# A fused decoder layer on one core: attention scores as three single-pass products, with the instruction lists written anew

## The reference, cut to what matters

```python
x = _layernorm(x + _L0_attn_ref(x, ...))                 # mixer
x = _layernorm(x + _L0_xattn_ref(ctx_1024, x, ...))      # attention
x = _layernorm(x + _L0_ffn_ref(x, ...))                  # three cycles
# the attention, 8 heads of 64; 120 context rows + 256 own rows = 376 keys
kv_input = jnp.concatenate([xn, ln], axis=-2)
q, k, v = (to_heads(q) * scale, to_heads(k), to_heads(v))
sim = jnp.einsum('bhid,bhjd->bhij', q, k)                # 256 x 376 scores a head
attn = jax.nn.softmax(sim, axis=-1)
out = jnp.einsum('bhij,bhjd->bhid', attn, v)
```

## Time and profile before

| | |
|---|---|
| median of 3 runs | 3804.09 us |
| profiled execution | 3802.06 us, of which the span is 3800.1 us |
| granted TensorE clock | mean 0.992; 1.00 (2.4 GHz) from 100 us on |
| busy in the span | PE 98%, PEld 79%, DVE 85%, ACT 87%, POOL 48% |
| DMA | 203 MB, 53 GB/s, 18% of the 16 DMA engines |

### The profile page before, as it was taken

The page is one execution under the profiler, slowest core; times in us unless marked ns, Lnnn a source line. Parts: engine busy times, 40 slices in busy tenths (PEclk is TensorE's granted clock), DMA queues, the critical chain, the costliest instruction groups (busy, mean ns, idle before and its releaser), DMA issues.

```text
span 3800.1 us, 77874 instructions
## 1 busy us (share of the span) xinstructions
PE 3718.5 (98%) x25728; PEld 2996.7 (79%) x25728; DVE 3248.2 (85%) x8098; ACT 3304.6 (87%) x7875; POOL 1810.0 (48%) x3084
## 2 busy tenths in 40 slices
PE   5999999999999999999999999999999999999996
PEld 4788887878878878888878788788888888787875
DVE  7888888888988888888888888888888888888874
ACT  5888988988888889889889898898898898888985
POOL 4355455454454554554554544545545545445442
PEclk8999999999999999999999999999999999999998
DMA  3111211212212212112112122121121121221210
GB/s 103 57 57 41 65 49 49 60 44 60 59 39 65 59 39 65 57 42 65 42 57 60 42 62 59 39 65 58 41 65 56 43 64 40 59 60 39 65 29 20
DMA packets 312353, 203.17 MB, mean 53 GB/s; under 512 B 55056, under 2 KB 310928, under 8 KB 311952
## 3 DMA queue, kind: packets, MB, share of 16 engines
q1 hardware_dynamic: 311952, 198.20, 18.0%
HBM read 180.17 MB, written 17.96 MB: 52 GB/s over the span
## 4 chain that ended last, share of the span: by engine, by line
PE 75%; ACT 19%; issue 2%; DVE 2%; POOL 1%; SPq 0%; DMA 0%; POOLq 0%; DVEq 0%; ACTq 0%
PE psum L254 28%; PE psum L453 9%; PE psum L429 8%; PE psum L439 7%; PE psum L464 6%; PE psum L498 5%; PE psum L326 5%; ACT prob L986 3%; PE psum L504 2%; ACT L986 2%; ACT L1028 2%; ACT L878 2%; PE psum L513 1%; ACT h L1028 1%; ACT gate L929 1%
## 5 line engine op out<-in xcount | busy, mean ns | idle before, releaser
L986 ACT ACTIVATE prob<-psum,nmax 128x376 f32<-128x376 f32 x1024 | 585.9, 573 | 60.6 <-DVE nmax L1686 57.2
L1686 DVE TENSOR_REDUCE nmax<-psum 128x1 f32<-128x376 f32 x1024 | 539.1, 537 | 36.7 <-PE psum L429 32.1
L2440 POOL TENSOR_TENSOR Lm<-Lm,G 128x384 f32<-128x384 f32 x512 | 526.9, 1064 | 87.2 <-DVE out_sb L1814 67.7
L439 PE MATMUL psum<-ident,prob 128*128 128x128 f32 (+1 forms) x3072 | 509.9, 278 | 3.3 <-ACT probT L996 1.1
L439 PEld LDWEIGHTS psum<-ident,prob 128*128 128x128 f32 (+1 forms) x3072 | 359.6, 143 | 169.5 <-issue 36.8
L1453 DVE SCALAR_TENSOR_TENSOR u<-psum,par,u 128x255 f32<-128x255 f32 (+5 forms) x960 | 440.0, 476 | 44.0 <-ACT u L888 29.5
L429 PE MATMUL psum<-kT,q_sb 64*128 64x376 f32 x2048 | 464.5, 528 | 0.0
L1709 DVE COPY probT<-psum 128x384 f32<-128x384 f32 x512 | 281.2, 549 | 125.5 <-PE psum L439 121.5
L2495 POOL TENSOR_TENSOR h_a<-h_a,cpl 128x512 f32<-128x512 f32 x64 | 82.3, 1285 | 611.0 <-DVE h_pre L1797 611.0
L254 PE MATMUL psum<-x_hi,w_in_hi 128*128 128x256 f32 (+1 forms) x1152 | 342.1, 297 | 26.5 <-DVE u L1453 15.3
L453 PE MATMUL psum<-probT,V 128*64 128x256 f32 (+1 forms) x3072 | 360.7, 383 | 0.6 <-DVE probT L1709 0.6
(11 more groups left out here) (220 smaller groups left out, 11350.5 us busy)
## 6 DMA issues: line engine op xcount, KB each, us to landing
Lm<-cum_row SPq DMA_DIRECT2D x64, 1024.0 KB, 5.2
Lm<-cum_row SPq DMA_DIRECT2D x64, 512.0 KB, 6.5
invT<-inv_row SPq DMA_DIRECT2D x256, 128.0 KB, 3.1
xT_sb<-in_xT SPq DMA_DIRECT2D x64, 256.0 KB, 2.9
x_sb<-in_x SPq DMA_DIRECT2D x64, 256.0 KB, 2.9
result<-out_sb SPq DMA_DIRECT2D x64, 256.0 KB, 2.2
inv_row<-inv_t SPq DMA_DIRECT2D x512, 1.0 KB
ctx_sb<-in_ctx SPq DMA_DIRECT2D x64, 120.0 KB, 4.2
```

The source lines that it names most:

```text
L439: t = tr(banks[b][0:m, j * P:(j + 1) * P], prob[:, r, j0:j0 + m], ident[:, :])
L986: act(prob[:, r, :], b[:, 0:NK], ACT.Exp, bias=nmax[:, n:n + 1], accum_out=psum_row[:, n:n + 1]).then_inc(a_exp, 1)
L1686: e.tensor_reduce(nmax[:, n:n + 1], banks[bank_of["sc", s, n]][:, 0:NK], AX.X, ALU.max, negate=True).then_inc(d_max, 1)
L2440: t = tt(Lm[:, h, :], Lm[:, h, :], G[:, :], ALU.mult)
```

## The change

- Scores: `k_out` and `q_out` now write float32r halves `k_hi` and `q_hi`; VectorE gets two new helpers, `k_low` (4 a sequence, 376 columns) and `q_low` (2 a sequence, 512 columns), which write the low halves and release the bank. `scores` makes three float32r products for each head, six matmuls in place of two, and tells of both tiles with one semaphore.
- `top` reduces the two tiles of a call at once (8 a sequence on 2 x 376 columns). `exp` stays at 16.
- `ring_s` has four banks, 0 to 3; the network's banks come from `ring_m`.
- `y_pair` puts two calls in one bank, and `values` does two pairs of heads with one bank and one release; `values_out` copies 512 columns, twice a sequence.
- `x1_pre` is gone: `x1_sum` writes into `x1[s % 2]`, which `x1_keep` normalises in place. `xT_sb` shares its memory with `x_lo`, and `kv` with `kv_lo`; `ctx_n` is `ctx_sb`, and `x_sb` is single. The loads and the copies that write them wait for later events.
- All lists of all engines are written in a new order.

```diff
+        def shared(name, other, shape):
+            at = -(-nc.sbuf_base // 32) * 32
+            t = sb(name, shape, F32R)
+            slices = tuple(slice(None) for _ in shape)
+            return t, nc.alloc_sbuf_tensor_at(other, shape, F32, offset=at)[slices]
...
-        xT_sb, x_sb = sb("xT_sb", [P, KT, L]), sb("x_sb", [P, 2, TT, D])
+        x_sb = sb("x_sb", [P, TT, D])
...
-        kv, kv_hi, kv_lo = sb("kv", [P, KT, NK]), sb("kv_hi", [P, KT, NK], F32R), sb("kv_lo", [P, KT, NK], F32R)
-        q_sb, kT = sb("q_sb", [P, CT, L]), sb("kT", [P, CT, NK])
+        kv_hi, (kv_lo, kv) = sb("kv_hi", [P, KT, NK], F32R), shared("kv_lo", "kv", [P, KT, NK])
+        q_hi, q_lo = sb("q_hi", [P, CT, L], F32R), sb("q_lo", [P, CT, L], F32R)
+        k_hi, k_lo = sb("k_hi", [P, CT, NK], F32R), sb("k_lo", [P, CT, NK], F32R)
...
-            ring_s, ring_b, ring_m = [1, 2, 3], list(ring_turn), [6, 7]
+            ring_s, ring_b, ring_m = [0, 1, 2, 3], list(ring_turn), [6, 7]
...
             def k_tile(s, c):
...
-                freed[b] = [(a_k, 4 * s + c + 1)]
+                freed[b] = [(d_kl, 4 * s + c + 1)]
...
             def scores(s, c, i):
-                pe.wait_ge(a_q, 2 * s + c // 2 + 1)
-                pe.wait_ge(a_k, 4 * s + c + 1)
+                pe.wait_ge(d_ql, 2 * s + c // 2 + 1)
+                pe.wait_ge(d_kl, 4 * s + c + 1)
+                at = [take(ring_s), take(ring_s)]
+                bank_of["sc", s, n // 2] = at[0]
+                assert at[1] == at[0] + 1
+                for m, (q_, k_) in enumerate(((q_hi, k_hi), (q_lo, k_hi), (q_hi, k_lo))):
+                    for k in range(2):
+                        r = slice(k * HD, (k + 1) * HD)
+                        t = mm(banks[at[k]][:, 0:NK], q_[r, c, i * P:(i + 1) * P], k_[r, c, :], start=m == 0, stop=m == 2)
+                t.then_inc(p_sc, 1)
                 for k in range(2):
-                    b = bank_of["sc", s, n + k] = take(ring_s)
-                    r = slice(k * HD, (k + 1) * HD)
-                    mm(banks[b][:, 0:NK], q_sb[r, c, i * P:(i + 1) * P], kT[r, c, :], start=True, stop=True).then_inc(p_sc, 1)
-                    freed[b] = [(a_exp, 16 * s + n + k + 1)]
+                    freed[at[k]] = [(a_exp, 16 * s + n + k + 1)]
...
             def layer(s, cyc, n):
-                b = wait_free(0)
+                at = bank_of["f", s, cyc, n] = take(ring_m)
+                b = banks[at]
...
-                act(oT[:, c, :], b[:, 0:L], ACT.Copy).then_inc(a_o, 1)
+                act(oT[:, 2 * d:2 * d + 2, :], b[:, :].rearrange("p (c t) -> p c t", c=2), ACT.Copy).then_inc(a_o, 1)
...
+            def q_low(s, j):
+                ve.wait_ge(a_q, 2 * s + j + 1)
+                tt(q_lo[:, 2 * j:2 * j + 2, :], b[:, :].rearrange("p (c t) -> p c t", c=2),
+                   q_hi[:, 2 * j:2 * j + 2, :].bitcast(F32), ALU.subtract).then_inc(d_ql, 1)
+            def k_low(s, c):
+                ve.wait_ge(a_k, 4 * s + c + 1)
+                tt(k_lo[:, c, :], banks[bank_of["k", s, c]][:, 0:NK], k_hi[:, c, :].bitcast(F32), ALU.subtract).then_inc(d_kl, 1)
...
-                e.tensor_reduce(nmax[:, n:n + 1], banks[bank_of["sc", s, n]][:, 0:NK], AX.X, ALU.max, negate=True).then_inc(d_max, 1)
+                e.tensor_reduce(nmax[:, 2 * n:2 * n + 2], psum[:, b:b + 2, 0:NK], AX.X, ALU.max, negate=True).then_inc(d_max, 1)
...
             def load_xT(s):
-                sp.wait_ge(d_xlo, s)
+                sp.wait_ge(p_bcdt, s)
+                sp.wait_ge(p_x, 2 * s)
+                sp.wait_ge(p_z, 2 * s)
```

More of the change, by code:

```diff
@@ new lines, in _ @@
+                v_tile(f, 0)
+                cb(a)
+                in_z(a, 1)
+                turn(f, 0)
+                w_o(f - 1, 0)
+                w_o(f - 1, 1)
+                turn(f, 1)
+                scores(f, 1, 0)
+                scores(f, 1, 1)
+                turn(f, 2)
+                q_pair(f, 1)
+                y_pair(a, 0)
+                y_pair(a, 1)
+                y_pair(a, 2)
+                y_pair(a, 3)
+                scores(f, 2, 0)
+                bcdt(m)
@@ new lines, in _ @@
+                k_tile(f, 3)
+                in_x(m, 0)
+                v_tile(f, 1)
+                x2_turn(f - 1)
+                turn(f, 3)
+                scores(f, 2, 1)
+                scores(f, 3, 0)
+                turn(f, 4)
+                turn(f, 5)
+                mean_square(a)
+                out_proj(a)
+                layer(f - 1, 0, 0)
+                v_tile(f, 2)
+                ctxT(a)
+                layer(f - 1, 0, 1)
+                turn(f, 6)
+                glob(f - 1, 0)
@@ L621, in _ @@
+                turn(f, 7)
+                layer(f - 1, 0, 2)
+                glob(f - 1, 1)
+                scores(f, 3, 1)
+                turn(f, 8)
+                glob(f - 1, 2)
+                twisted(f - 1)
+                layer(f - 1, 0, 3)
+                turn(f, 9)
+                turn(f, 10)
+                x1T(a)
+                in_x(m, 1)
+                values(f, 0)
+                k_tile(a, 0)
+                layer(f - 1, 1, 1)
+                q_pair(a, 0)
                 layer(f - 1, 1, 2)
@@ L685, in _ @@
-                values(a, 0)
-                values(a, 1)
-                q_pair(m, 0)
-                layer(f, 1, 1)
-                turn(a, 10)
-                k_tile(m, 0)
-            last = NSEQ - 1
+            last = NSEQ - 1
+            values(last - 3, 1)
+            layer(last - 4, 2, 3)
+            cb(last - 1)
+            v_tile(last - 2, 0)
+            in_z(last - 1, 1)
+            scores(last - 2, 1, 0)
+            turn(last - 2, 0)
+            w_o(last - 3, 0)
+            q_pair(last - 2, 1)
@@ new lines, in _ @@
+            w_o(last - 3, 1)
+            scores(last - 2, 1, 1)
+            y_pair(last - 1, 0)
+            y_pair(last - 1, 1)
+            scores(last - 2, 2, 0)
+            y_pair(last - 1, 2)
+            y_pair(last - 1, 3)
+            bcdt(last)
+            turn(last - 2, 1)
+            turn(last - 2, 2)
+            in_x(last, 0)
+            k_tile(last - 2, 3)
+            v_tile(last - 2, 1)
+            x2_turn(last - 3)
+            turn(last - 2, 3)
+            scores(last - 2, 2, 1)
@@ new lines, in _ @@
+            scores(last - 2, 3, 0)
+            turn(last - 2, 4)
+            turn(last - 2, 5)
+            mean_square(last - 1)
+            out_proj(last - 1)
+            layer(last - 3, 0, 0)
+            turn(last - 2, 6)
+            v_tile(last - 2, 2)
+            ctxT(last - 1)
+            layer(last - 3, 0, 1)
+            turn(last - 2, 7)
+            turn(last - 2, 8)
+            glob(last - 3, 0)
+            layer(last - 3, 0, 2)
+            glob(last - 3, 1)
+            scores(last - 2, 3, 1)
@@ L692, in _ @@
+            glob(last - 3, 2)
+            twisted(last - 3)
+            layer(last - 3, 0, 3)
+            turn(last - 2, 9)
+            turn(last - 2, 10)
+            x1T(last - 1)
+            in_x(last, 1)
+            values(last - 2, 0)
+            k_tile(last - 1, 0)
+            layer(last - 3, 1, 1)
+            q_pair(last - 1, 0)
             layer(last - 3, 1, 2)
             k_tile(last - 1, 1)
+            layer(last - 3, 1, 3)
+            turn(last - 2, 11)
             xcT(last, 0)
-            layer(last - 3, 1, 3)
+            xcT(last, 1)
@@ L707, in _ @@
             layer(last - 3, 2, 2)
-            values(last - 2, 2)
-            values(last - 2, 3)
-            scores(last - 1, 0, 1)
-            turn(last - 1, 0)
+            values(last - 2, 1)
             layer(last - 3, 2, 3)
@@ new lines, in _ @@
+            conv_tap(last, 2, 2)
+            k_low(last - 1, 0)
+            x_silu(last, 0)
+            q_low(last - 1, 0)
+            x_silu(last, 1)
+            out_stats(last - 4, 0)
+            k_low(last - 1, 1)
+            gain(last - 3, 1)
+            x_dt(last, 0)
+            twisted_part(last - 3, 1)
+            turn_inverse(last - 2, 1)
+            pre(last - 3, 1)
+            turn_out(last - 2, 12)
+            k_low(last - 1, 2)
+            top(last - 1, 0)
+            x_dt(last, 1)
```

1578 lines of the change are left out of this document (733 added, 845 removed).

## The result

The changed kernel takes 3687.03 us (median of 4 runs, 3685.63 to 3689.21), the kernel before 3804.62 (4 runs, 3803.94 to 3806.9): ratio 0.969, 95% interval 0.9674 to 0.9707. It is 117.6 us faster.

What follows compares the result with a forecast made beforehand. PE, full of work, was taken as the bound: 3802 us less 96 (products 64, shapes 32) plus 32 of new waits gives 3738, forecast as a median of 3740 us, range 3690 to 3840.

Steps and rivals of the forecast that it cites:

- Products, 64 us: Score calls on PE: three rounds of float32r products at 0.17 us, saving 0.125 us a call, 64 us in all.
- Both float32r rivals: Score calls slower: float32r halves don't run abreast (3969 us, chance 5%), or each round shows its weight load (3998, 2%).
- The lists at 32 us: New order of PE's loop: 15 changes of array shape a sequence instead of 18, saving 32 us (0 to 45).
- PE, fewer changes of shape: Prediction's step on PE's loop: three fewer changes of array shape a sequence at 0.165 us each, 32 us saved.
- no room for a wait: PE's timeline before the change: matmul starts follow so closely that PE is full of work, 57.9 us a sequence.
- Waits, +32 us: PE waiting for DVE's new low halves at scores and banks: 0.5 us a sequence more, 32 us (0 to 141).
- more gain: Rival on PE: rounds of 0.157 us, no new waits, bank waits gone; 3675 to 3690 us, chance 6%.
- ACT at nothing: ScalarE: 236 us of table loads and 23 of values_out copies come off, but none counts in the sum.
- DVE +142 us: VectorE: k_low adds 138 us, q_low 87, merged maxima take 83 off; net 142, 94% busy.
- DVE's waits eat the gain: Rival: PE's gain is eaten by waits for DVE, whose idle time falls to 3.5 us a sequence; 3800 to 3945, 17%.
- Memory, at nothing: Loads and shared buffers: later input load (2.9 us), in-place x1 and single x_sb stay covered and cost nothing.
- One microsecond taken off PE's list is worth 64 us: PE as the bound: each microsecond less of PE work a sequence shortens the kernel by 64 us.

Runs made afterwards that it cites:

- joined_y: The changed kernel with the joined score calls of the second pair of heads moved behind a turn and q_pair, just ahead of y_pair: 3806.19 us.
- x_low_early: The changed kernel with x_low(m) on VectorE moved from behind y_out(a, 0) to ahead of gate_silu(a, 1): 3738.46 us.
- two_products: The changed kernel with the third product of each score tile (q_hi by k_lo) left out: 3671.75 us.

## Why the prediction was wrong

- **Products, 64 us: right.** 0.119 us a call instead of 0.125, 61 us. Both float32r rivals fell, and with them what the Trainium skill's rule on weight loads ("TensorE: Matmul & The Clock Gate", "The mechanism") would have given: loads of the same rows of the array are hidden in the halves too.
- **The lists at 32 us: the step that failed.** "PE, fewer changes of shape" took the lists' worth to be the count of changes, 3 x 0.165 us, and nothing else. The changes themselves came out near that: the three joined score pairs save 0.61 us a sequence and the joined `y_pair` 0.15, while 0.20 is lost where both calls of `values` are now followed by a change back to the full array (before, one of them was followed by a score call). That is 0.56 us, 36 us in all. But the lists brought 71 us by the records and 76 by the runs. The largest other part is `v_tile`, 0.49 us a sequence (31 us): its three calls ended 1.55, 1.40 and 1.83 us after the group before them, and end after 1.38, 1.40 and 1.49 now. I had read PE's starts as leaving "no room for a wait", and so had no term for waits that the old lists held. The row of the slowest `v_tile`, the one behind `glob`, shows one, and its first record is 0.1 us longer than its equals besides (for the 1.55 no row names a wait):

```profile
2007.90 0.50 PE L254 MATMUL psum<-wkv_hi,kv_hi 128*128 128x512 f32 x1 [0.16 <-ACT probT L996]
2008.24 0.40 PE L254 MATMUL psum<-wkv_lo,kv_hi 128*128 128x512 f32 x1
2008.48 0.40 PE L254 MATMUL psum<-wkv_hi,kv_lo 128*128 128x512 f32 x1
```

- **Waits, +32 us: wrong in size and in place.** New waits are 0.3 us a sequence (19 us, from 61 on PE to 42 in the runs), and the old ones at `v_tile` went. Where I had PE's waits rising by 32 us in sum, they fell. This and the step before make the 53 us between 3740 and 3687: the lists gave 44 more than forecast, the new waits took 13 less, the products gave 3 less (the rest is rounding).
- **The rival "more gain" (3675 to 3690) holds the measured time, but not by its reasons.** Rounds are 0.171 us and not 0.157, there are new waits, and the wait for a bank in the earlier trace rows was rare: that call takes 0.86 us on average where the others take 0.83, 2 us in the whole run.
- **ACT at nothing: wrong.** 241 us came off as table loads (188 of them; the forecast's 184 left out four) and 25 at `values_out`, while other copies and exponentials took some 35 us longer: 232 in sum. Loading the table 2 or 4 times more a sequence costs 38 and 200 us; in the kernel before 2 more cost 235. The new lists with the 8 loads of the kernel before weren't run; between 7 and 9 they lose 38 to 200 us, so I infer that without ScalarE's relief a large part of the 117 us would not have come. How large stays open.
- **DVE +142 us: right in its parts, wrong in its sum.** The parts are k_lo 0.544 us x 256, q_lo 0.688 x 128, merged maxima 0.934 x 512, as forecast within 3%:

```profile
L1733 DVE TENSOR_TENSOR k_lo<-psum,k_hi 128x376 fp32r<-128x376 f32 x256 | 139.2, 544 | 33.6 <-ACT k_hi L996 32.7
L1726 DVE TENSOR_TENSOR q_lo<-psum,q_hi 128x512 fp32r<-128x512 f32 x128 | 88.1, 688 | 4.8 <-ACT q_hi L988 4.7
L1741 DVE TENSOR_REDUCE nmax<-psum 128x2 f32<-128x752 f32 x512 | 472.8, 934 | 44.2 <-PE psum L443 39.4
```

 What I had no term for: the new order parts instructions that GpSimd had slowed. x_lo went from 1.20 to 0.68 us on average (33 us in all), ncum from 0.32 to 0.17 (39 us), `out_sb<-x,of_x` from 0.52 to 0.35 (22 us). In the kernel before x_lo overlapped `Lm<-Lm,G` in 61 of 64 sequences and ncum `affine_select` in 247 of 256 cases. With smaller savings of this kind the durations of all instructions rise by 36 us, and the busy time, in which overlapping records count once, by nothing.
- **The rival "DVE's waits eat the gain" fell** as an account of the change (DVE idles 5.7 us a sequence, not 3.5), but its mechanism is real: `joined_y` and `x_low_early` lost 119 and 51 us by one late instruction on VectorE's queue.
- **Memory, at nothing: right.** x_sb now lands in 5.8 us (2.9 before) and the context in 6.4 (4.2), unseen by PE.
- **"One microsecond taken off PE's list is worth 64 us": wrong for the changed kernel.** `two_products` took 1.37 off and gained 0.24.

## What to carry to other kernels

An engine at 99% busy isn't proof that it sets the pace: its records can span waits. Sum by group how long each takes from the end of the one before, compare with the shortest of the same shape, and you see them. In a software pipeline with in-order queues, ask of every engine how much could be added to it before PE is late; ScalarE at 87% had no room here. A hand-over that waits can be moved by exchanging two neighbours on a queue, but whoever stands behind them has to be moved too.
